# Seven block products in place of eight in the up half of a shared feed-forward network, with operand sums on GpSimd and token routing moved later

## The chip, the cores and the metric

The kernel runs on one core of a Trainium2 chip. The metric is device time in microseconds (us), from the start to the end of one execution. The engines are named as in the profile: PE (TensorE) multiplies matrices, DVE (VectorE) and ACT (ScalarE) work element by element, POOL (GpSimd) does so too and issues gathers and scatters, SP (SyncE) issues the other DMA transfers. Each engine works through its own list of instructions in order and stops at a wait until a semaphore has the value wanted.

## The reference

Inputs are x (2 x 2048 x 512, so 4096 tokens of width 512), a condition vector per batch, and weights. The tokens are first projected by a conditioned 512 x 512 matrix. Then each token goes through a shared two-layer network (512 to 2048 to 512) and through one of two routed networks of the same size, chosen by a gate, and the sums are added to x:

```python
xf = conditioned_projection(x, cond)             # 4096 x 512
top1 = argmax(softmax(xf @ gate_w.T))
shared = relu(xf @ sw1 + sb1) @ sw2 + sb2        # the part that is changed: relu(xf @ sw1 + sb1)
routing = relu(xf @ w1[top1] + b1[top1]) @ w2[top1] + b2[top1]
out = x + routing + shared
```

(Rows of the expert that was not chosen are zero at its input, but still give relu(b1) @ w2 + b2; the kernel adds this as a constant row.)

## The kernel before, in words

Every fp32 product is made of three matmuls: an operand a is split into a high part (rounded to fp32r) and a low part (a minus the high part), and high*high, high*low and low*high are summed. ACT makes the high parts (a cast), DVE the low parts (a subtraction).

The work goes in four stages, one after the other on PE.

1. Projection (line L1722): 32 chunks of 128 tokens, 12 matmuls each. SP loads x into `ring`, ACT and DVE split it, ACT or DVE takes the result from PSUM into `xo`, DVE forms the gate score (L1171), SP stores it to DRAM as xf (L518). Meanwhile the first weights of the shared network are loaded (`raw_load`, L492), cast (`raw_hi`, L834) and subtracted (`raw_lo`, L1201), and the first block of 1024 tokens is read back (`rows`, L524), transposed on DVE (`flip`, L1221) and split into `xw` (`block_hi` L848, `block_lo` L1227).
2. Up half of the shared network (L1776): four blocks s of 1024 tokens, four groups g in each, numbered u = 4s + g from 0 to 15. A group makes relu(xf @ sw1 + sb1) for 4 of the 16 slices of 128 hidden columns. These are two rows (h) by two pairs (p). Together with the two halves (t) of 512 tokens and the two halves (q) of the 512 inputs this is a 2 x 2 by 2 x 2 block product; a group computes it directly, in four steps c (`UP_STEPS`, L79) with 2 x 12 matmuls each. ACT takes each PSUM bank with bias and relu into `vb11`, `vb21`, `vt1` and `vb22` (L932). DVE makes from these the operands of the next stage, t1 to t4, by four subtractions of 128 x 1024 (L1300, L1310, L1263, L1268), and SP stores all seven (512 KB each, L536) to DRAM. In groups 0 to 2 the rest of the weights of sw1 are loaded and split; in groups 8 to 15 (`RAW_JOBS`, L85) those of sw2, with the sums that stage 3 needs. Each block's `rows` are loaded in group g = 1 of the block before (`next_rows`, L528), flipped in g = 2 and split in g = 3 and in the next g = 0. The routing (softmax, choice, counts, places: L1330 to L1418) stands in DVE's list in groups 0 and 1, the scatter of the token table on POOL (L692) in groups 3 to 6.
3. Down half of the shared network (L1811): seven block products per 1024 tokens instead of eight, from the seven stored operands and seven combinations of the weights.
4. The routed networks (L1846, L1870), then the scatter of the results.

PSUM has eight banks, `turn` is four pairs of them. Step c of a group uses pair c, and PE waits before step c only until ACT has taken what step c of the group before left there (L1769). ACT in turn waits for the stores of two groups before (L929) and the subtractions of the group before (L930), since each buffer but `vt3` and `vt4` is there twice.

In the prediction, "c0 to c6" are the seven products of a group of the changed kernel, each with two halves p = 0, 1 of six matmuls.

Of the kernel before, what the change touches and what calls it, by code (L numbers as in the profile page):

```python
# [12 lines left out]
P = 128  # L13
# [15 lines left out]
RAW_AT = (18, 25)  # L29
FLIP_AT = (20, 22, 24, 26)  # L30

LOAD_AT = (4, 20, 27)
ROWS_AT = (10, 12, 14, 16)
# [25 lines left out]
RANK_GROUP = 1  # L59
SCATTER_GROUP = 3  # L60
# [18 lines left out]
UP_STEPS = ((0, 0), (1, 0), (0, 1), (1, 1))  # L79
# [5 lines left out]
RAW_JOBS = {0: (2, 3, 4), 1: (5, 6), 2: (7,), 8: (8, 9), 9: (10,), 10: (11,), 11: (12,), 12: (13, 14), 13: (15, 16, 17), 14: (18, 19),  # L85
            15: (20, 21)}

EARLY = {(3, 4): 0, (3, 7): 1}
# [33 lines left out]
def build(nc, x_rows, x_cols, cond, w_cond, w_shared, w_pack, b1_pack, sb2_cols, b2_rows, gate, out):  # L122
# [4 lines left out]
    with ExitStack() as ctx:  # L127
# [57 lines left out]
        w_raw = at(40, "w_raw", [KD, D])  # L185
        scratch = at(104, "scratch", [KD, D])
        junk = at(38, "junk", [D])
        x_hi = at(128, "x_hi", [KD, T], F32R)
        x_lo = at(136, "x_lo", [KD, T], F32R)
        ring = at(144, "ring", [RING, D])  # L190
# [3 lines left out]
        gate_w = at(96, "gate_w", [2, D])  # L194
        d_rows = at(100, "d_rows", [D])
# [3 lines left out]
        vb11 = [at(kb, f"vb11_{i}", [2, T]) for i, kb in enumerate((128, 56))]  # L199
        vt1 = [at(kb, f"vt1_{i}", [2, T]) for i, kb in enumerate((132, 148))]  # L200
        vb22 = [at(kb, f"vb22_{i}", [2, T]) for i, kb in enumerate((136, 60))]
        vb21 = [at(kb, f"vb21_{i}", [2, T]) for i, kb in enumerate((140, 120))]
        vt2 = [at(kb, f"vt2_{i}", [2, T]) for i, kb in enumerate((144, 124))]
        vt3 = at(204, "vt3", [2, T])
        vt4 = at(200, "vt4", [2, T])
        xw = at(152, "xw", [4, 2, 2, T], F32R)
        rows = at(184, "rows", [JW, QF])
        raw = at(208, "raw", [4, 256])
        raw_last = [at(kb, f"raw_last{i}", [4, 256]) for i, kb in enumerate((160, 164))]
        sums = at(212, "sums", [3, 256])  # L210
        rank = at(104, "rank", [2, NT])
        scan = at(104.5, "scan", [2, NT])
        place = at(105, "place", [4, NT])
        ids = at(106, "ids", [NT * IDW], I32)
# [35 lines left out]


# [6 lines left out]
        raw_in = sem("raw_in")  # L258
        raw_last_in = [sem(f"raw_last_in{i}") for i in range(2)]
# [1749 lines left out]
```

## Time and profile before

| | us |
|---|---|
| median of 3 runs | 1463.8 (1463.56 to 1463.91) |
| span of the profiled execution | 1461.8 |
| projection, to the first up matmul | 97.0 |
| up half, first to last matmul | 97.0 to about 445.7 |
| down half | 445.7 to about 751 |
| routed networks and end | the rest |

Readings of the profile: "busy" is the time that an engine had an instruction in work; "idle before" is the time that it waited in front of a group of instructions, with what ended the wait. The chain is followed back from the last instruction of the kernel, at each step to what released it.

### The profile page before, as it was taken

How to read it: one execution, taken by the hardware profiler on the slowest of the kernel's cores; microseconds unless marked ns; L12 is line 12 of the kernel's file. 1: busy time of each engine (PE TensorE's matmuls, PEld its weight loads, DVE VectorE, ACT ScalarE, POOL GpSimd, SP SyncE). 2: the span in 40 equal slices, each digit the busy share in tenths (PEclk: the TensorE clock that was granted, in tenths of full speed). 3: DMA queues.
4: the chain of work that ended last, by engine and by line, in shares of the span. 5: the costliest groups of instructions: out<-in, count | busy, mean ns of one | idle time of the engine just before them, and what ended most of it. 6: DMA issues, size and time to landing. Idle time of an engine off the chain costs nothing.

```text
span 1461.8 us, 17696 instructions
## 1 busy us (share of the span) xinstructions
PE 1455.4 (100%) x6454; PEld 1207.6 (83%) x6454; DVE 739.2 (51%) x1206; ACT 454.1 (31%) x724; POOL 313.4 (21%) x354
## 2 busy tenths in 40 slices
PE   9999999999999999999999999999999999999998
PEld 8888888888888888888888888888888888888886
DVE  7853723444437877777874514324245531423235
ACT  4353322323336444444533211111124211111112
POOL 0000233210001110000033240614215151340533
PEclk9999999999999999999999999999999999999999
DMA  6947675695678897977675220312106221120312
GB/s 214 283 143 220 222 207 200 194 267 204 213 261 311 283 296 260 288 251 238 204 223 172 60 49 12 66 20 47 40 10 205 60 58 30 29 57 2 66 22 33
DMA packets 157445, 219.87 MB, mean 150 GB/s; under 512 B 46816, under 2 KB 63712, under 8 KB 157376
## 3 DMA queue, kind: packets, MB, share of 16 engines
q1 hardware_dynamic: 142496, 190.90, 40.7%
q0 software_dynamic: 14880, 28.07, 9.5%
q8 instruction: 40, 0.66, 0.2%
q14 instruction: 29, 0.24, 0.0%
HBM read 135.39 MB, written 85.75 MB: 151 GB/s over the span
## 4 chain that ended last, share of the span: by engine, by line
PE 98%; POOL 0%; issue 0%; DVE 0%; DMA 0%; POOLq 0%; DVEq 0%
PE bank L1776 24%; PE bank L1846 24%; PE bank L1870 23%; PE bank L1811 21%; PE bank L1722 6%; PE bank L1866 0%; PE bank L1699 0%; POOL out L735 0%; PE bank L1705 0%; DMA out<-res,tab 0%; POOL out L738 0%; DVE res L1621 0%; POOLq L127 0%; DVE res L1662 0%; DVEq L127 0%
## 5 line engine op out<-in xcount | busy, mean ns | idle before, releaser
L1776 PE MATMUL bank<-xw,w_hi 128*128 128x512 f32 x1024 | 315.5, 389 | 0.0
L718 POOL DMA_INDIRECT rows_e<-xf_scratch,soft x144 | 143.4, 996 | 724.3 <-PE bank L1811 323.3
L1811 PE MATMUL bank<-hl,w_hi 128*128 128x512 f32 x896 | 275.7, 389 | 0.0
L1023 ACT ACTIVATE hf<-bank,b 128x512 f32<-128x512 f32 (+1 forms) x128 | 87.2, 681 | 547.8 <-PE bank L1846 457.6
L1595 DVE CAST h_hi<-hf 128x512 fp32r<-128x512 f32 (+1 forms) x128 | 56.9, 444 | 387.7 <-ACT hf L1023 331.5
L1776 PEld LDWEIGHTS bank<-xw,w_hi 128*128 128x128 f32 x1024 | 192.1, 188 | 39.8
L1776 PE MATMUL bank<-xw,w_lo 128*128 128x512 f32 x512 | 199.2, 389 | 0.0
L1846 PE MATMUL bank<-xe_lo,w_hi 128*128 128x512 f32 (+1 forms) x512 | 197.7, 386 | 0.0
L1846 PE MATMUL bank<-xe_hi,w_hi 128*128 128x512 f32 (+1 forms) x512 | 197.6, 386 | 0.0
L1811 PEld LDWEIGHTS bank<-hl,w_hi 128*128 128x128 f32 x896 | 168.2, 188 | 34.9
L1846 PE MATMUL bank<-xe_hi,w_lo 128*128 128x512 f32 (+1 forms) x512 | 196.0, 386 | 0.0
L1870 PE MATMUL bank<-w_lo,h_hi 128*128 128x512 f32 x496 | 193.0, 389 | 0.0
L1870 PE MATMUL bank<-w_hi,h_hi 128*128 128x512 f32 x496 | 193.0, 389 | 0.0
L1870 PE MATMUL bank<-w_hi,h_lo 128*128 128x512 f32 x496 | 193.0, 389 | 0.0
L898 ACT CAST hl<-hin 128x512 fp32r<-128x512 f32 x224 | 137.6, 621 | 147.2 <-PE bank L1811 123.3
L1256 DVE TENSOR_TENSOR hl<-hin,hl 128x512 fp32r<-128x512 f32 x224 | 147.7, 686 | 63.8 <-ACT hl L898 63.3
L1811 PE MATMUL bank<-hl,w_lo 128*128 128x512 f32 x448 | 174.3, 389 | 0.0
L932 ACT ACTIVATE vb<-bank,b 128x512 f32<-128x512 f32 x96 | 65.7, 690 | 152.0 <-PE bank L1776 149.5
L1776 PEld LDWEIGHTS bank<-xw,w_lo 128*128 128x128 f32 x512 | 96.1, 188 | 20.0
L1846 PEld LDWEIGHTS bank<-xe_lo,w_hi 128*128 128x128 f32 x512 | 96.2, 188 | 18.7
L1846 PEld LDWEIGHTS bank<-xe_hi,w_hi 128*128 128x128 f32 x512 | 96.1, 188 | 18.8
L1846 PEld LDWEIGHTS bank<-xe_hi,w_lo 128*128 128x128 f32 x512 | 96.0, 188 | 18.4
(208 smaller groups left out, 1566.9 us busy)
## 6 DMA issues: line engine op xcount, KB each, us to landing
hin<-hidden_scratch SPq DMA_DIRECT2D x112, 512.0 KB
hidden_scratch<-vt SPq DMA_DIRECT2D x64, 512.0 KB, 3.1
hidden_scratch<-vb SPq DMA_DIRECT2D x48, 512.0 KB, 5.1
stage<-w_pack SPq DMA_DIRECT2D x64, 256.0 KB
raw<-w_shared SPq DMA_DIRECT2D x44, 256.0 KB
ring<-x_cols SPq DMA_DIRECT2D x32, 256.0 KB, 4.2
xf_scratch<-xo SPq DMA_DIRECT2D x32, 256.0 KB, 3.8
rows<-xf_scratch SPq DMA_DIRECT2D x16, 512.0 KB, 9.3
```

The source lines that it names most:

```text
L718: pool.indirect_dma_start(rows_e[:, c % JN, :], None, xf_dram, bass.IndirectOffsetOnAxis(tab_rows[:, c:c + 1], 0)).then_inc(rows_gathered, ...
L898: nc.scalar.copy(hl[:, n % HL, 0, :], hin[:, n // 2 % LOADS, n % 2, :]).then_inc(hu_hi, 1)
L932: nc.scalar.activation(dst[:, p, :], turn[c][p][:], ACT.Relu, bias=b1[:, 0, n:n + 1]).then_inc(up_relu, 1)
L1023: nc.scalar.activation(hf[:, j % 2, 0:width(u)], hidden_bank(j, first and e > 0)[:, 0:width(u)], ACT.Relu, bias=b1[:, 1 + e, j:j + 1]).the ...
L1256: nc.vector.tensor_tensor(hl[:, n % HL, 1, :], hin[:, n // 2 % LOADS, n % 2, :], hl[:, n % HL, 0, :].bitcast(F32), ALU.subtract).then_inc( ...
L1595: nc.vector.tensor_copy(h_hi[:, buf, 0:filled_n], hf[:, j % 2, 0:filled_n]).then_inc(hh_ready, 4)
L1722: last = nc.tensor.matmul(p_ps[c % P_BANKS][:], lhs[:, k, i * P:(i + 1) * P], rhs[:, 24 + 4 * b + k, :], start=(k == 0 and q == 0), stop=( ...
L1776: last = nc.tensor.matmul(turn[c][p][:], w[:, 2 * h + q, 2 * g + p, part], xw[:, 2 * t + q, x, k, :], start=(n == 1), stop=(n == 12))
L1811: last = nc.tensor.matmul(bank[p][:], w[:, DOWN_W[c], i, part], hl[:, n % HL, h, :], start=(i == 0 and q == 0), stop=(i == PAIRS - 1 and q ...
L1846: last = nc.tensor.matmul(hidden_bank(j, change)[:, 0:width(u)], w_of(lhs, lhs3, j, j + 1)[:, 0, part], rhs[:, k, 0:width(u)], start=(k == ...
L1870: last = nc.tensor.matmul(y_ps[m][:], lhs[:, j % HB, part], w_of(rhs, rhs3, j, j + 1)[:, 0, D:2 * D], start=(j == 0 and q == 0), stop=(j = ...
```

## The change

The up half is computed by seven block products per group instead of eight. With b11, b12, b21, b22 for the blocks of x, the kernel makes four sums of them on POOL (`x_sums`), and three sums of the weight blocks (`raw_sums`, also moved from DVE to POOL). Each product c has its own split operand in `xw` (seven of them, not four, so seven `block_hi` and `block_lo` per block), and six matmuls per half, not twelve. Products 0, 2, 4 and 6 of a group run into one and the same pair of banks (`UP_BANK`), without clearing it: ACT takes the bank after 0, after 2 and after 6, DVE adds what stands there after 4 to `vb22`; 1 and 5 share a second pair, 3 has a third. So the results are no longer taken with relu directly: ACT takes 0, 1 and 2 with the bias alone, DVE adds products 3, 4 and 5 to them from PSUM (`add`, six of 128 x 512), ACT applies relu to `vb11` and `vb22` in place (two of 128 x 1024), and relu for `vt1` is within t1's subtraction. `vt1`, `vb22`, `vb21` and `vt2` are there only once; t3 is made in place in `vb11`, t4 in `vb21`.

Before c2 PE waits for ACT's take of c0, before c4 for that of c2, before c5 for that of c1, before c6 for DVE's add of c4, and before c3 for DVE's add of c5 in the group before.

Weights of sw1 and sw2 are now loaded once each into the first buffer (16 loads, not 22). The choice of the expert moves to group 4, the counting to group 5, the places to group 8, the scatter to groups 9 to 11 and the reading of the table to group 12. In the projection, loads, flips and splits come at other chunks, and buffers move to other addresses.

Most lines that are only removed are left out of the diff; they stand in the functions above.

```diff
-RAW_AT = (18, 25)
-FLIP_AT = (20, 22, 24, 26)
-LOAD_AT = (4, 20, 27)
-ROWS_AT = (10, 12, 14, 16)
+RAW_AT = (13, 17)
+FLIP_AT = (18, 19, 20, 21)
+X_AT = (22, 24, 26, 28, 30)
+LOAD_AT = (4, 14, 18)
+ROWS_AT = (9, 11, 12, 13)
...
-RANK_GROUP = 1
-SCATTER_GROUP = 3
+CHOOSE_GROUP = 4
+RANK_GROUP = 5
+PLACE_GROUP = 8
+SCATTER_GROUP = 9
+TABLE_GROUP = 12
...
-UP_STEPS = ((0, 0), (1, 0), (0, 1), (1, 1))
+UP_BANK = (0, 1, 0, 2, 0, 1, 0)
+FRESH = (0, 1, 3)
+PER_GROUP = 2 * STEPS
+X_ORDER = (0, 1, 3, 2, 4, 5, 6)
+X_DONE = tuple(X_ORDER.index(c) + 1 for c in range(STEPS))
+X_EARLY = 5
+X_SUM = (None, 1, 3, None, 2, None, 4)
...
+RAW_JOBS = {0: (2, 3), 1: (4, 5), 2: (6, 7), 13: (8, 9), 14: (10, 11), 15: (12, 13)}
+RAW_FIRST = {0: (4,), 1: (6,), 12: (8, 9), 13: (10, 11), 14: (12, 13)}
+RAW_SECOND = {0: (3,), 1: (5,), 2: (7,)}
...
+                home = RAW_HOME[n]
+                if RAW_USE[n]:
+                    before_n = max(m for m in range(n) if RAW_HOME[m] == home)
+                    sp.wait_ge(raw_ready, before_n + 1)
+                    sp.wait_ge(sums_made, 4 * (before_n + 1))
...
+                    last = u == GROUPS * BLOCKS - 1
+                    if last:
+                        for n in range(LOADS - 1):
+                            hidden_load(n)
+                    if u > 0:
+                        keep_t3(u - 1)
                     if g == 1 and s < BLOCKS - 1:
                         next_rows(s)
+                    for n in RAW_SECOND.get(u, ()):
+                        raw_load(n)
                     if u > 0:
...
+                        keep_t4(u - 1)
+                    sp.wait_ge(b11_made, u + 1)
                     keep(vb11[u % 2][:], s, g, 0).then_inc(b11_out[u % 2], DMA)
...
+                    sp.wait_ge(b22_made, u + 1)
+                    keep(vb22[:], s, g, 5).then_inc(b22_out, DMA)
+                    for n in RAW_FIRST.get(u, ()):
                         raw_load(n)
...
+            def x_sums(s):
+                b11_x, b12_x, b21_x, b22_x = half_of(0, 0), half_of(0, 1), half_of(1, 0), half_of(1, 1)
+                pool.wait_ge(x_flip, FLIPS * (s + 1))
+                pool.wait_ge(xw_lo, STEPS * s + X_DONE[0])
+                pool.tensor_tensor(b11_x, b12_x, b11_x, ALU.subtract).then_inc(x_sum, 1)
+                pool.wait_ge(x_sum, 4 * s + 1)
+                pool.tensor_tensor(b12_x, b22_x, b12_x, ALU.subtract).then_inc(x_sum, 1)
+                pool.wait_ge(xw_lo, STEPS * s + X_DONE[1])
+                pool.tensor_tensor(b11_x, b22_x, b11_x, ALU.subtract).then_inc(x_sum, 1)
+                pool.wait_ge(x_sum, 4 * s + 3)
+                pool.wait_ge(xw_lo, STEPS * s + X_DONE[3])
+                pool.tensor_tensor(b21_x, b21_x, b11_x, ALU.subtract).then_inc(x_sum, 1)
+            for n in range(3):
+                raw_sums(n)
+            x_sums(0)
+            for n in range(3, PAIRS):
+                raw_sums(n)
+            x_sums(1)
...
             pool.wait_ge(pads_out, 2 * DMA)
...
+            def block_hi(s, i):
+                c = X_ORDER[i]
                 act.wait_ge(x_flip, FLIPS * (s + 1))
+                if X_SUM[c]:
+                    act.wait_ge(x_sum, 4 * s + X_SUM[c])
                 if s > 0:
...
+                    act.wait_ge(up_mm, PER_GROUP * (GROUPS * s - 1) + 2 * c + 2)
                 nc.scalar.copy(in_blocks(xw[:, c, 0, :, :]), X_OF[c]).then_inc(xw_hi, 1)
             act.wait_ge(fills_made, 2)
...
+                def take(dst, c, h, f):
                     for p in range(2):
...
+                        nc.scalar.activation(dst[:, p, :], up_bank(u, UP_BANK[c])[p][:], f, bias=b1[:, 0, n:n + 1]).then_inc(up_kept, 1)
+                if u == CHOOSE_GROUP:
                     act.wait_ge(soft_in, 3)
                     nc.scalar.activation(soft[:, 3:5, :], soft[:, 1:3, :], ACT.Exp).then_inc(soft_exp, 1)
+                wait(act, t3_out[u % 2], DMA * (u // 2))
+                take(vb11[u % 2], 0, 0, ACT.Identity)
+                if g == 0:
+                    for i in range(X_EARLY, STEPS):
+                        block_hi(s, i)
+                if more:
+                    block_hi(s + 1, 0)
                 for n in jobs[:1]:
                     raw_hi(n)
...
+                take(vb22, 1, 1, ACT.Identity)
+                for n in jobs[:1]:
+                    raw_sums_hi(n)
+                if last:
+                    first_units(0, 2)
+                wait(act, t1_out, DMA * u)
+                take(vt1, 2, 0, ACT.Identity)
...
+                for n in jobs[1:]:
                     raw_hi(n)
                 if last:
...
+            def make_t1(u):
+                dve.wait_ge(b11_made, u + 1)
+                dve.wait_ge(up_added, 6 * u + 6)
+                nc.vector.scalar_tensor_tensor(out=vt1[:], in0=vt1[:], scalar=0.0, in1=vb11[u % 2][:], op0=ALU.max,
+                                               op1=ALU.subtract).then_inc(ht_made, 1)
+            def make_t2(u):
+                dve.wait_ge(b22_made, u + 1)
+                dve.wait_ge(ht_made, 4 * u + 1)
+                wait(dve, t2_out, DMA * u)
+                nc.vector.tensor_tensor(vt2[:], vb22[:], vt1[:], ALU.subtract).then_inc(ht_made, 1)
...
+                dve.wait_ge(b11_out[u % 2], DMA * (u // 2 + 1))
                 dve.wait_ge(ht_made, 4 * u + 2)
...
             def make_t4(u):
...
+                dve.wait_ge(b21_out, DMA * (u + 1))
+                dve.wait_ge(up_kept, 8 * u + 8)
+                nc.vector.tensor_tensor(vb21[:], vb21[:], vt2[:], ALU.subtract).then_inc(ht_made, 1)
...
+                more = g == GROUPS - 1 and s < BLOCKS - 1
+                def add(dst, c, kept, p):
+                    dve.wait_ge(up_mm, PER_GROUP * u + 2 * c + p + 1)
+                    dve.wait_ge(up_kept, 8 * u + kept + p + 1)
+                    nc.vector.tensor_tensor(dst[:, p, :], up_bank(u, UP_BANK[c])[p][:], dst[:, p, :], ALU.add).then_inc(up_added, 1)
+                if u == CHOOSE_GROUP:
+                    softmax_start()
+                if g == 0:
+                    for i in range(X_EARLY, STEPS):
+                        block_lo(s, i)
...
+                for n in jobs[:1]:
+                    raw_lo(n)
+                    raw_sums_lo(n)
+                if u == CHOOSE_GROUP:
...
+                    slots()
+                if u == PLACE_GROUP:
                     places()
...
+                if u > 0:
+                    make_t4(u - 1)
+                if more:
                     block_lo(s + 1, 0)
                     block_lo(s + 1, 1)
...
+                if last:
+                    units_lo(0, 2)
+                add(vb11[u % 2], 3, 0, 0)
+                add(vb11[u % 2], 3, 0, 1)
+                for n in jobs[1:]:
+                    raw_lo(n)
+                add(vb22, 4, 2, 0)
+                if more:
+                    block_lo(s + 1, 2)
+                add(vb22, 4, 2, 1)
+                if more:
+                    block_lo(s + 1, 3)
+                for n in jobs[1:]:
+                    raw_sums_lo(n)
+                add(vt1, 5, 4, 0)
+                add(vt1, 5, 4, 1)
+                if more:
+                    block_lo(s + 1, 4)
                 if u == 0:
                     for i in range(RING):
                         dve.wait_ge(xf_out[i], DMA * NT // RING)
...
+                if last:
+                    units_lo(2, 4)
+                make_t1(u)
+                if last:
+                    raw_lo(RAW_LAST)
...
+                            pe.wait_ge(raw_ready, pair + 1)
+                        if s == 0 and c == 2:
+                            pe.wait_ge(sums_ready, pair + 1)
+                        if c == 0:
+                            wait(pe, up_added, 6 * (u - 2) + p + 1)
+                        elif c == 1:
+                            wait(pe, up_kept, 8 * (u - 1) + 6 + p + 1)
+                        elif c == 2:
+                            pe.wait_ge(up_kept, 8 * u + p + 1)
+                        elif c == 3:
+                            wait(pe, up_added, 6 * (u - 1) + 4 + p + 1)
+                        elif c == 4:
+                            pe.wait_ge(up_kept, 8 * u + 4 + p + 1)
+                        elif c == 5:
+                            pe.wait_ge(up_kept, 8 * u + 2 + p + 1)
+                        else:
+                            pe.wait_ge(up_added, 6 * u + 2 + p + 1)
                         n = 0
...
+                        for k in range(2):
+                            part = slice(k * P, (k + 1) * P)
+                            for w, x in ((w8_hi, 0), (w8_hi, 1), (w8_lo, 0)):
+                                n += 1
+                                last = nc.tensor.matmul(up_bank(u, UP_BANK[c])[p][:], w[:, DOWN_W[c], pair, part], xw[:, c, x, k, :],
+                                                        start=(c in FRESH and n == 1), stop=(n == 6), skip_group_check=(c not in FRESH))
                         last.then_inc(up_mm, 1)
                     if u == RANK_GROUP and c == 0:
```

## Rows read from the trace of the kernel before

**Rows 1.** The page: the span and each engine's busy time, share, instructions

```profile
span 1461.8 us, 17696 instructions
...
PE 1455.4 (100%) x6454; PEld 1207.6 (83%) x6454; DVE 739.2 (51%) x1206; ACT 454.1 (31%) x724; POOL 313.4 (21%) x354
```

**Rows 2.** Waits of PE: engine, line waited for, us, times, longest

```profile
PE bank L1699 <- POOL ones L664: 1.2, 1, 1.2
```

**Rows 3.** The chain that ended last: start us, length us, what ran

```profile
1.19 4.33 PE bank L1699 x10
...
124.77 321.09 PE bank L1776 x1416
```

**Rows 4.** Line L1776: duration ns min/median/max, first and last start us, forms

```profile
L1776 PE MATMUL bank<-xw,w_hi x1024: 387/389/477, 97.0 to 445.2; 128*128 128x512 f32 x171
...
L1776 PE MATMUL bank<-xw,w_lo x512: 389/389/397, 97.5 to 445.5; 128*128 128x512 f32 x171
```

**Rows 5.** Groups by shape: operation, shapes, count, busy us, mean ns, idle, releaser

```profile
L932 ACT ACTIVATE vb<-bank,b 128x512 f32<-128x512 f32 x96 | 65.7, 690 | 152.0 <-PE bank L1776 149.5 <-DVE vt L1310 2.0
...
L1310 DVE TENSOR_TENSOR vt<-vb,vt 128x1024 f32<-128x1024 f32 x16 | 19.6, 1225 | 48.8 <-ACT vb L932 48.6
...
L1225 DVE STREAM_TRANSPOSE rows<-rows 128x1024 f32<-128x1024 f32 x16 | 18.8, 1220 | 0.0
...
L1210 DVE TENSOR_TENSOR w_lo<-raw,w_hi 128x1024 fp32r<-128x1024 f32 x14 | 17.2, 1225 | 36.8 <-ACT w_hi L838 27.1 <-ACT w_hi L846 9.4
L853 ACT CAST xw<-rows 128x1024 fp32r<-128x1024 f32 x16 | 16.1, 1047 | 0.0
L1488 DVE TENSOR_TENSOR v<-bank,v 128x512 f32<-128x512 f32 x24 | 15.4, 684 | 0.3
...
L1210 DVE TENSOR_TENSOR w_lo<-sums,w_hi 128x768 fp32r<-128x768 f32 x8 | 7.7, 958 | 7.2 <-ACT w_hi L841 7.2
...
L706 POOL TENSOR_SCALAR soft<-soft 128x144 int32<-128x144 int32 x1 | 0.7, 697 | 0.1
...
L686 POOL IOTA ids<- 128x512 int32 x1 | 0.7, 656 | 32.1 <-DVE w_lo L1158 32.1
```

**Rows 6.** Groups of POOL in 0 to 110 us

```profile
L673 POOL IOTA order<- 128x32 f32 x1 | 0.2, 156 | 0.0
```

**Rows 7.** ACT in order of time, first block group: start us, us, engine, line

```profile
100.04 0.69 ACT L932 ACTIVATE vb<-bank,b 128x512 f32<-128x512 f32 x1 [1.27 <-PE bank L1776]
...
103.39 1.28 ACT L940 ACT_TABLE_LOAD   x1
104.68 0.26 ACT L940 ACTIVATE soft<-soft 128x64 f32<-128x64 f32 x1
...
142.48 1.05 ACT L838 CAST w_hi<-raw 128x1024 fp32r<-128x1024 f32 x1 [11.41 <-DMA raw<-w_shared]
```

**Rows 8.** DVE in order of time, the routing steps

```profile
124.80 0.22 DVE L1351 COPY rank<-bank 128x64 f32<-128x64 f32 x1 [1.36 <-PE bank L1785]
...
144.70 0.15 DVE L1392 TENSOR_SCALAR filled<-scan 128x1 f32<-128x1 f32 x1
...
151.78 0.19 DVE L1408 TENSOR_TENSOR place<-scan,rank 128x32 f32<-128x32 f32 x1
...
158.06 1.22 DVE L1300 TENSOR_TENSOR vt<-vt,vb 128x1024 f32<-128x1024 f32 x1
```

**Rows 9.** SP in order of time: start us, us of issuing, what

```profile
119.68 6.42 SPq L532 DMA_DIRECT2D rows<-xf_scratch  x4
...
131.60 1.10 SPq L507 DMA_DIRECT2D raw<-w_shared  x2
```

**Rows 10.** Windows of 2 us: PE, PEld, DVE, ACT, POOL, PEclk, DMA share, GB/s

```profile
131.00:133.00 2.00, 2.00 (x11) 1.65 (x10) 0.00 (x0) 0.06 (x1) 0.00 (x0) 1.00 1.22 218
133.00:135.00 2.00, 2.00 (x11) 1.65 (x10) 0.00 (x0) 0.00 (x0) 0.00 (x0) 1.00 1.02 382
```

**Rows 11.** Line L536, the stores of halves: us from issue to landing

```profile
DMA to landing us min/median/max: 2.8/3.5/11.6
```

More of the change, by code:

```diff
@@ L249, in down_bank, with up_bank, wc_tile, sums_of @@
             return turn[(STEPS * s + c) % TURN]
+        def up_bank(u, role):
+            return turn[(3 * u + role) % TURN]
+        def wc_tile(b, k):
+            return 28 + k if b else 4 * k + 3
+        def sums_of(n):
+            return sums if n < 2 * PAIRS - 1 else sums_last
         const_in = sem("const_in")
@@ L942, in up_group @@
                     raw_hi(n)
-                relu(vb21[u % 2], b21_out, 1)
-                for n in jobs[1:2]:
-                    raw_hi(n)
-                if s < BLOCKS - 1 and g == GROUPS - 1:
-                    block_hi(s + 1, 0)
+                wait(act, b22_out, DMA * u)
+                wait(act, ht_made, 4 * (u - 1) + 2)
+                take(vb22, 1, 1, ACT.Identity)
[3 more added lines that the diff above has]
+                    first_units(0, 2)
@@ L958, in _ @@
+                if last:
+                    first_units(6, HL)
+                if u == 0:
+                    for i in range(RING):
+                        act.wait_ge(xf_out[i], DMA * NT // RING)
+                wait(act, t4_out, DMA * u)
+                take(vb21, 6, 1, ACT.Relu)
             act.wait_ge(tile_mm, NT)
@@ L1272, in up_group @@
                 jobs = RAW_JOBS.get(u, ())
-                b11, b21, b22, t1, t2 = (x[u % 2] for x in (vb11, vb21, vb22, vt1, vt2))
-                if s > 0 and g == 0:
-                    block_lo(s, 2)
-                    block_lo(s, 3)
-                for n in jobs[:2]:
-                    if n == PAIRS - 1:
-                        raw_job(n)
-                if s < BLOCKS - 1 and g == 2:
+                last = u == GROUPS * BLOCKS - 1
+                more = g == GROUPS - 1 and s < BLOCKS - 1
@@ L1300, in up_group @@
[L1300 to L1310 removed]
+                if last:
+                    units_lo(0, 2)
@@ L1359, in count, with slots @@
                     a = 1 - a
-            def places():
+            def slots():
                 total = scan[:, 1, NT - 1:NT]
@@ L1764, in up_group @@
                         pe.wait_ge(rank_kept, 1)
                     for p in range(2):
+                        pair = 2 * g + p
                         if s == 0 and c == 0:
[L1768 to L1777 removed]
+                            pe.wait_ge(raw_ready, pair + 1)
```

445 lines of the change are left out of this document (192 added, 253 removed).

## The prediction

> **What bounds the kernel now.** First the page: PE is busy for 1455.4 of 1461.8 us [rows 1]. Then its waits, to see whether that is real work: its only wait is 1.2 us at the start [rows 2]. Then the chain that ended last: in the up half it is PE alone, 1416 matmuls in 321.09 us, 0.2268 us each [rows 3] (the 389 ns of a single matmul [rows 4] overlap with the next). Six matmuls take 1.36 us, twelve 2.72. So PE's instruction count sets the time, and whatever else happens between 97 and 446 us is hidden. The question is what stops being hidden.
>
> **What goes.** A group had 4 x 2 x 12 = 96 matmuls and will have 7 x 2 x 6 = 84; over 16 groups 1536 [rows 4] become 1344. 192 x 0.2268 = 43.5 us less, if PE never waits. A group then lasts 84 x 0.2268 = 19.05 us. The stages before and behind keep their matmuls. Six weight loads and DVE's weight sums go too; they were hidden, 0.
>
> **What comes, in a plain group.** I count from the group's start; product cj ends at 2.72(j+1), its first half 1.36 earlier, and ACT or DVE start about 0.3 us later (the first take began at 100.04, 2.72 + 0.3 behind 97.0 [rows 7]). Prices: a take 0.69, an add from PSUM 0.68, a DVE operation of 128x1024 1.22, of 128x768 0.96, an ACT cast of 128x1024 1.05 [rows 5]; I take relu in place at 1.05 too.
> ACT: 8 takes and 2 relus = 7.6 us of 19.05, before 5.5. DVE: 6 adds and 4 subtractions = 9.0, before 4.9. Both fit; the order counts, as PE now waits within the group. Take c0 ends at 2.4, needed at 5.44; take c2 at 7.8, needed at 10.9; add of c4's first half at 13.2, needed by c6 at 16.3. Everywhere about 3.1 us in hand, where before it was nearly a whole group (ACT once sat 11.41 us on a load [rows 7], and PE never noticed [rows 2]). Ahead of the adds in DVE's list is t4 of the group before, which waits for b21's store: taken at 20.05, so 1.0 into the next group, landing 3.5 us later [rows 11], t4 ends at 5.8; c3's add is due from 9.8. t1 is stored at about 18.7 and lands at 22.2, 3.2 into the next group, where ACT wants the buffer at 7.1. In groups 5 and 9 t4's store stands behind `rows` in SP's list (t3 at 2.1, rows to about 13), lands by 16, and ACT wants the buffer at 18: 0. The single buffers cost nothing at 3.5 us. So a plain group costs 0; what follows are the groups with extra work.
>
> **Projection, 0.** Five block splits and two pairs of weight splits in place of four and two, on engines that PE leads by up to four chunks (10.9 us).
>
> **Group 0, 0.3 us.** Weight load 3 goes out when `raw_lo(2)` is done (8.6), lands at 12, two sums on POOL (0.7 each, below), cast 1.05, subtraction 1.22, then the add for c6: 16.3 to 16.7 against 16.3.
>
> **Group 1, 7 us.** SP issues t3's store, then the four `rows` loads, then weight load 5. t3 of group 0 is made at about 23, 4 into group 1. The rows run at 205 to 218 GB/s until 133 us and the stores behind them at 382 [rows 10]; 2.1 MB are 10 us. In the kernel before, the load issued at 131.60 behind rows issued from 119.68 [rows 9] was there only at 142.48 [rows 7], 22.8 us after the first rows, with some 7 stores besides (1.3 us each). Here about 2 us of stores, 10 of rows and 1.3 + 1.4 of its own: it lands 15 us after 4, at about 19. Two sums, cast, `raw_lo(5)` and the add follow (1.4 + 1.05 + 1.22 + 0.7), 23.3, against 16.3: 7 us. `raw_lo(5)` stands in DVE's list before c4's add, and `raw_hi(5)` in ACT's before the relus, so all of them wait. Bounds 4 (t3 earlier, queue empty) and 10 (queue full).
> **Group 2, 1.3 us.** DVE is 4 us late, then 4 flips (4.9), split of 6, load 7 out at 9.9, landing 13.3, the same 4.4: 17.7 against 16.3.
>
> **Change of block (groups 3, 7, 11), 0 in the group itself, but DVE ends late.** Five of seven splits are made in the old block's last group, with POOL's sums between. The trace has no POOL operation with two inputs. Nearest rows: iota takes 156 ns for 32 columns and 656 for 512 [rows 5, 6], 1.04 ns a column; with two inputs I take twice that, 2.3 us for 1024 and 0.7 for 256. Bounds: 1.2 (as DVE) and 5 (the int32 TENSOR_SCALAR, 697 ns for 144 columns [rows 5], scaled). With 2.3: block split 0 ends at 7.0, sum 1 at 9.3, its cast 10.4, its subtraction 11.6, sum 3 at 13.9, and the last split at 18.9; t1, t2, t3 end at 22.6, 3.6 into the next group. PE's operands are all in time (c1 of the next block at 21.8, c2 at 24.5). If instead DVE's subtractions and POOL's sums don't overlap but take turns, each chain link grows by up to 1.2 to 2.3, and DVE ends 7.0 late. No row shows two-input work of both at a time; I take the middle, 5.3.
> The Trainium skill, "SBUF — State Buffer", section "Who interferes with whom", says that a DVE instruction with two SBUF inputs and a GpSimd instruction that reads SBUF lock each other out; by it the lateness is 7.0 and the sum 3.5 us larger, 1439; without it 2.7 us less. Its page "GPSIMD Engine Reference" (section "Elementwise — side-by-side cycle accounting") gives 4497 ns for 2048 columns, an estimate of 2.25 us here. No run here shows either yet.
>
> **Group 4, 2.7 us.** ACT's list begins with the Exp, which waits for DVE's `softmax_start`, which stands behind t3: 5.3 + 0.5, then table load and Exp 1.28 + 0.26 [rows 7], then take c0: 8.1 against 5.44 for c2. Bounds 1.0 and 9 (POOL at 5 us).
> **Group 5, 0.2.** Count about 2.0 from 124.80, `slots` 7.1 (144.70 to 151.78) [rows 8], from 3.9 on; then t4 and three adds: 16.3 to 16.5.
> **Group 8, 1.0.** 5.3 late, splits 5 and 6 (2.4), places 6.3 (151.78 to 158.06 [rows 8]), t4 1.2, three adds 2.1: 17.3 against 16.3. Bounds 0 and 7.4.
> **Scatter, table, weights of sw2, 0**: POOL only, or 4.4 us of DVE per group with 7 us free, no rows in the queue from group 12 on.
> **Into the down half, 0.3.** Unit 6 is split at 26.7 against 27.2, unit 7 at 28.6 against 28.6.
> **Clock, 2.1.** After idleness the first ten matmuls took 4.33 us in place of 2.27 [rows 3], 2.1 more. I charge that once, for the 7 us gap; 0 and three times are the bounds.
>
> **Sum.** 0.3 + 7 + 1.3 + 2.7 + 0.2 + 1.0 + 0.3 + 2.1 = 14.9. Span 1461.8 - 43.5 + 14.9 = 1433.2. The median of the runs stands 2.0 above the span: 1435.2.
>
> **Rivals.**
> *The covers hold.* The weight load overtakes or t3 comes early, POOL is fast: 0 to 8 us lost, 1463.8 - 43.5 + 4 = 1424. For it: 3 us in hand everywhere and an unloaded store of 3.5 us. Against: SP's order in group 1 is fixed.
> *DVE and POOL take turns* (the rule above): DVE ends block changes 7.0 late, group 4 loses 4.5 and group 8 2.8, 1438.8; if they overlap in full 3.6 late, 1.1 and 0, 1432.5. For the first: the chain cast, subtraction, sum leaves them back to back; against: no row has them together. I hold them equally likely; both lie within the forecast's case.
> *POOL is slow.* At 5 us a sum DVE ends block changes 11.7 late: group 4 loses 9, group 8 7.4, three block changes 4 together, with the 8.9 of groups 0 to 2, 5 and the end, and three clock prices 6.3: 36 us, 1456. For it: the int32 row. Against: that row has few columns, much of it may be fixed.
> *Slower: the single buffers bind in every group.* b21's store must land before t4, t4 precedes the adds: 1.1 + L + 1.2 + 2.1 reaches 16.3 at a landing L of 11.9 us. Each us beyond costs 16, so from L = 14.6 on the gain is gone; L = 16 gives 1463.8 - 43.5 + 4.1 x 16 = 1486. For it: the same bytes in less time, and a largest landing of 11.6 [rows 11]. Against: the median is 3.5, and a group's stores need 7 x 1.3 = 9 of 19 us.
>
> **Chances.** Forecast (1428 to 1444) 0.50, half of it with turns, half without; covers hold (1420 to 1428) 0.28; slow POOL (1444 to 1462) 0.15; binding stores 0.07. The forecast is the first. The range 1422 to 1450 holds it, most of the second and the near part of the third. 0.2% (3 us) is about what a measurement can tell from no change: faster 0.92; same 0.02, from the ends of the last two cases; slower 0.06.
>
> **What would show it.** 1344 matmuls in the up half at 0.2268 us; PE's waits: one of 5 to 10 us in group 1, ended by a DVE add behind `raw_lo`, one of 1 to 5 in group 4, near 189 us, in front of c2, ended by ACT's take, one of up to 3 in group 8; plain groups 6, 9, 10 and 13 to 15 at 19.05 us. POOL's 128x1024 sums at 2.3 us; 3.5 us landing for the stores. Wrong would be: no wait in group 1 (the queue isn't in order, or t3 earlier), waits in each group (stores or ACT's length), or sums of over 3 us.

## The result and the profile after

| | before | after |
|---|---|---|
| median of the runs | 1463.9 us (1463.6 to 1463.9) | 1507.0 us (1504.9 to 1510.9) |
| ratio to before, 95% interval | | 1.0296 [1.0284, 1.0309] |
| span of the profiled execution | 1461.8 us | 1504.9 us |
| PE busy, matmuls | 1455.4 us, 6454 | 1428.1 us, 6262 |
| mean granted clock | 1.00 | 0.978 |

The change made the kernel 3% slower; 1435.2 was forecast, in 1422 to 1450. The page of the profile shows that the matmuls went, and the tenths show where the time came back.

```profile
span 1504.9 us, 17708 instructions
...
PE 1428.1 (95%) x6262; PEld 1177.5 (78%) x6262; DVE 830.8 (55%) x1282; ACT 502.0 (33%) x776; POOL 406.9 (27%) x434
...
PE   9897889999549999999999999999999999999998
```

PE's instructions fell by 192 as planned, yet its busy time fell only from 1455.4 [rows 1] to 1428.1, 27.3 us in place of 43.5. The third line is PE's busy share in 40 slices of 37.6 us: the "54" are the slices from 376 to 451 us, about half empty. The waits of PE (engine, line, what it waited for: us in total, times, longest):

```profile
PE bank L1889 <- ACT vt L998: 35.7, 3, 35.4
PE bank L1889 <- DVE vb L1356: 20.6, 8, 11.0
PE bank L1889 <- ACT vb L998: 4.9, 2, 3.4
PE bank L1926 <- DVE hl L1317: 4.6, 1, 4.6
PE bank L1817 <- DVE x_lo L1180: 4.3, 1, 4.3
```

Before, the only wait was the 1.2 us at the start [rows 2]. Together with one of 0.2 these are 70.3 us. PE in order of time shows the five longest (start, us, what, and in brackets the idle time before it and its releaser):

```profile
74.53 0.79 PE L1817 MATMUL bank<-w_hi,x_hi 128*128 128x512 f32 x1 [4.28 <-DVE x_lo L1180]
...
154.42 1.22 PE L1889 MATMUL bank<-xw,w_hi 128*128 128x512 f32 x2 [11.02 <-DVE vb L1356]
...
209.28 1.19 PE L1889 MATMUL bank<-xw,w_hi 128*128 128x512 f32 x2 [3.39 <-ACT vb L998]
...
432.77 1.22 PE L1889 MATMUL bank<-xw,w_hi 128*128 128x512 f32 x2 [35.35 <-ACT vt L998]
...
492.09 1.15 PE L1926 MATMUL bank<-hl,w_hi 128*128 128x512 f32 x2 [4.64 <-DVE hl L1317]
```

They are the projection, group 1, group 4, group 13 and the start of the down half.

**The account closes.** Without any loss the span would be 1461.8 - 43.5 = 1418.3, with PE busy for 1455.4 - 43.5 = 1411.9. Whatever PE waits for comes on top, and so does what its busy time exceeds 1411.9 by. After: 70.3 of waits and 1428.1 - 1411.9 = 16.2 of excess give 1504.8; the span is 1504.9. This is bookkeeping: PE is either busy or waits, so the account must close. What it gives is the split into waits and slower work, and it is used for every run below.

What the excess is, the windows show (PE, PEld, DVE, ACT, POOL, then PEclk, the DMA share and GB/s):

```profile
432.00:434.00 2.00, 1.23 (x3) 1.04 (x4) 1.84 (x2) 1.29 (x3) 0.74 (x1) 0.50 0.00 0
434.00:436.00 2.00, 2.00 (x6) 1.52 (x6) 1.45 (x3) 0.26 (x1) 1.84 (x3) 0.50 0.45 161
436.00:438.00 2.00, 2.00 (x7) 1.58 (x6) 1.18 (x1) 2.00 (x3) 1.20 (x2) 0.60 0.29 110
```

The granted clock is 0.50, the 1.2 GHz level, at the end of group 13's wait and for some 4.8 us behind it, and 1.00 (2.4 GHz) in a plain group. At 0.50 PE starts a matmul every 0.43 us in place of 0.227, so 4.8 us there cost 47% of that, 2.3. The same windows behind the other long gaps show 0.50 for 4.7 us (projection), 3.3 (group 1), 3.0 (group 4), 3.0 (group 8, behind a gap of 2.73) and 3.5 (down half). Behind the gap of 2.33 in group 0 it stays at 1.00. By the same 47% the six cost 10.5 us, an estimate. The other 5.7 of the excess I have not divided further; in e11 below, where the mean granted clock is 1.000, 5.4 us of excess are left, which points to a part of about that size that is not the clock.

### The profile page after: what moved, and what is told of

It is laid out like the page before. It is cut to its first block, busy times and chain, and to the rows that moved or that the text cites. A ratio compares the mean times of both kernels' runs of the same rounds, so it can differ in the third digit from the quotient of the medians.

```text
span 1504.9 us, 17708 instructions
## 1 busy us (share of the span) xinstructions
PE 1428.1 (95%) x6262; PEld 1177.5 (78%) x6262; DVE 830.8 (55%) x1282; ACT 502.0 (33%) x776; POOL 406.9 (27%) x434
## 4 chain that ended last, share of the span: by engine, by line
PE 71%; issue 4%; DVE 2%; DMA 2%; POOL 2%; ACT 0%; POOLq 0%; SPq 0%; DVEq 0%; ACTq 0%
PE bank L1961 23%; PE bank L1985 22%; PE bank L1926 20%; PE bank L1889 5%; DMA hin<-hidden_scratch 1%; POOL soft L770 1%; PE bank L1981 0%; DVE xw L1290 0%; DMA hidden_scratch<-vb 0%; DMA soft<-token_table 0%; DVE vb L1356 0%; DVE vt L1332 0%; POOL out L804 0%; POOL tab L767 0%; DVE vt L1324 0%
## 5 line engine op out<-in xcount | busy, mean ns | idle before, releaser
L1889 PE MATMUL bank<-xw,w_hi 128*128 128x512 f32 x896 | 282.9, 397 | 61.3 <-ACT vt L998 35.7
L1889 PEld LDWEIGHTS bank<-xw,w_hi 128*128 128x128 f32 x896 | 170.3, 192 | 102.5 <-ACT vt L998 36.4
L1889 PE MATMUL bank<-xw,w_lo 128*128 128x512 f32 x448 | 176.5, 394 | 0.0
L1985 PEld LDWEIGHTS bank<-w_hi,h_lo 128*128 128x128 f32 x496 | 93.1, 188 | 19.3
L1985 PEld LDWEIGHTS bank<-w_lo,h_hi 128*128 128x128 f32 x496 | 93.2, 188 | 19.2
```

What stands on the lines that cost most here:

```text
L1889: last = nc.tensor.matmul(up_bank(u, UP_BANK[c])[p][:], w[:, DOWN_W[c], pair, part], xw[:, c, x, k, :], start=(c in FRESH and n == 1), sto ...
L1985: last = nc.tensor.matmul(y_ps[m][:], lhs[:, j % HB, part], w_of(rhs, rhs3, j, j + 1)[:, 0, D:2 * D], start=(j == 0 and q == 0), stop=(j = ...
```

## What held group 13

POOL in order of time, from the end of the last `x_sums` on:

```profile
367.77 1.30 POOL L767 DMA_DIRECT2D tab<-token_table  x1
372.27 1.18 POOL L770 DMA_DIRECT2D soft<-token_table  x1 [3.20 <-issue]
...
417.77 1.12 POOL L770 DMA_DIRECT2D soft<-token_table  x1 [3.44 <-issue]
421.81 0.33 POOL L774 TENSOR_SCALAR tab_in<-tab 128x36 int32<-128x36 int32 x1 [2.93 <-DMA soft<-token_table]
...
427.58 0.72 POOL L723 TENSOR_TENSOR sums<-raw 128x256 f32<-128x256 f32 x1 [2.08 <-issue]
428.38 0.72 POOL L725 TENSOR_TENSOR raw<-raw 128x256 f32<-128x256 f32 x1
```

And ACT behind it:

```profile
429.19 1.04 ACT L914 CAST w_hi<-raw 128x1024 fp32r<-128x1024 f32 x1 [39.21 <-POOL raw L725]
```

Ten reads of the token table, issued by POOL (each takes 2304 single numbers of 4 bytes out of rows of 64), are each busy for 1.1 to 1.3 us, and between one and the next lie 3 to 7 us with nothing that the profile shows to wait for ("issue"): 54 us from the first to the table's use. In the kernel before the same ten were issued from 250 to 303 us, hidden. Its first and its last:

```profile
249.96 1.28 POOL L698 DMA_DIRECT2D tab<-token_table  x1 [1.42 <-DMA token_table<-ids,pos]
...
302.71 1.12 POOL L701 DMA_DIRECT2D soft<-token_table  x1 [8.83 <-issue]
```

Now the sums of the sw2 weights, which group 13 is the first to need, are behind them in POOL's list. ACT's cast waits 39 us for them and holds the takes behind it, and PE waits 35 us for a bank that only a take empties. No engine is overloaded here (POOL is 27% busy); it is the order of one list.

## Experiments

No run leaves out part of the computation. Medians, ratios to the kernel before on the same chip, and the account:

| run | median us | ratio [95%] | PE waits | excess | 1418.3 + both | span |
|---|---|---|---|---|---|---|
| after | 1507.0 | 1.0296 [1.0284, 1.0309] | 70.3 | 16.2 | 1504.8 | 1504.9 |
| e1 | 1470.2 | 1.0032 [1.0019, 1.0046] | 34.4 | 14.6 | 1467.3 | 1467.4 |
| e2 | 1503.7 | 1.0278 [1.0261, 1.0295] | 66.9 | 15.8 | 1501.0 | 1501.0 |
| e3 | 1497.5 | 1.0229 [1.0212, 1.0246] | 59.9 | 16.3 | 1494.5 | 1494.8 |
| e4 | 1459.5 | 0.9971 [0.9961, 0.9980] | 30.4 | 15.1 | 1463.8 | 1463.8 |
| e5 | 1451.6 | 0.9906 [0.9884, 0.9928] | 19.9 | 13.3 | 1451.5 | 1451.4 |
| e6 | 1454.1 | 0.9938 [0.9922, 0.9954] | 21.1 | 13.5 | 1452.9 | 1453.0 |
| e7 | 1451.8 | 0.9915 [0.9898, 0.9932] | 21.8 | 13.3 | 1453.4 | 1453.5 |
| e8 | 1498.2 | 1.0223 [1.0202, 1.0244] | 62.4 | 15.3 | 1496.0 | 1496.2 |
| e9 | 1441.5 | 0.9840 [0.9827, 0.9853] | 11.9 | 8.3 | 1438.5 | 1438.6 |
| e10 | 1440.4 | 0.9835 [0.9822, 0.9848] | 14.9 | 6.6 | 1439.8 | 1440.0 |
| e11 | 1443.5 | 0.9868 [0.9850, 0.9886] | 14.1 | 5.4 | 1437.8 | 1438.0 |

(PE waits without the 1.2 us at the start, which the kernel before has too. Waits, excess and span are those of the one execution that was profiled, which need not be a typical one: e4's is the slowest of its ten, 1465.8 us against a median of 1459.5, e11's the fastest of its four. Single waits also differ between runs whose code is the same up to them: the wait in the projection is 4.28 us in the changed kernel, 5.79 in e1 and 4.58 in e3. A difference of some 3 us between two medians is within the intervals.)

### e1: the weight sums ahead of the table reads

```diff
+            for n in range(PAIRS, 2 * PAIRS):
+                raw_sums(n)
-            pool.wait_ge(up_mm, PER_GROUP * TABLE_GROUP)
 ...
-            for n in range(PAIRS, 2 * PAIRS):
-                raw_sums(n)
```

> The changed kernel with one edit: POOL makes the sums of the sw2 weights (n = 8 to 15) before it reads the token table back, not after. Theory A (POOL's order is the cause): ACT's first weight cast of group 13 waited for POOL, which was busy with ten table reads from 367.8 to 421.7 us, and PE waited 35.35 us behind it and then ran some 6 us at the lower clock. Without it the wait is gone: 1507 - 35 - 3 = 1469, and no PE wait over 5 us after group 8. Rival B (the weight loads themselves are late, held by the scatter or by the stores in the queue): 1500 to 1507, the wait stays with POOL's first sum ended by a DMA. Rival C (the table is then late for the gathers of the routed networks): the wait is gone in the up half but one of 10 to 40 us comes at the start of the routed part, 1480 to 1507.

The edit also drops the wait that held the reads until group 12; it could not bind any more, since the reads now come behind the last sums, at 450 us. POOL of this run:

```profile
387.51 1.14 POOL L723 TENSOR_TENSOR sums<-raw 128x256 f32<-128x256 f32 x1 [20.25 <-DMA raw<-w_shared]
...
450.47 1.30 POOL L768 DMA_DIRECT2D tab<-token_table  x1
```

Measured 1470.2. The first sum is 40 us earlier than in the changed kernel (427.58), as soon as its load is there. PE's waits fall from 70.3 to 34.4; the one of 35 us is gone, and the only one that grew by more than 0.3 us is that of the projection (4.28 to 5.79), which the edit does not touch. This one order costs 37 us, nearly half of the 86.6 that the span lost against 1418.3. Theory A holds. Rival B falls, since the load was there at 387, and rival C too: the reads run to after 500 us now, and no wait of PE comes in the routed part.

### e2: weight load 1 ahead, in the projection

```diff
-RAW_AT = (13, 17)
+RAW_AT = (13, 20)
-LOAD_AT = (4, 14, 18)
+LOAD_AT = (4, 14, 21)
```

> The changed kernel with the second weight split of the projection three chunks later (chunk 20, not 17) and the third load behind it (21, not 18). Theory A (load 1 stands in the queue behind the four rows loads, ACT waits 6.10 us for its sums and holds up x's split): the 4.28 us wait of PE at 74.5 and the slow clock behind it go, first up matmul at 97 to 98, 1507 - 7 = 1500. Rival B (DVE is held up by POOL's x sums, the gate score took 2.89 us beside one): the start of the up half stays at 103 to 104.5, 1505 to 1507.

Measured 1503.7, not clear of noise against 1507.0. The wait at 74.5 us went, and one of 5.1 us came 20 us later. PE, POOL and DVE of this run:

```profile
95.04 0.79 PE L1817 MATMUL bank<-w_hi,x_hi 128*128 128x512 f32 x1 [5.09 <-DVE x_lo L1180]
```

```profile
85.38 0.73 POOL L723 TENSOR_TENSOR sums<-raw 128x256 f32<-128x256 f32 x1 [12.15 <-DMA raw<-w_shared]
...
88.52 2.36 POOL L736 TENSOR_TENSOR rows<-rows 128x1024 f32<-128x1024 f32 x1
90.95 2.35 POOL L738 TENSOR_TENSOR rows<-rows 128x1024 f32<-128x1024 f32 x1
```

```profile
92.04 2.34 DVE L1290 TENSOR_TENSOR xw<-rows,xw 128x1024 fp32r<-128x1024 f32 x1 [6.73 <-ACT xw L929]
94.31 0.68 DVE L1180 TENSOR_TENSOR x_lo<-ring,x_hi 128x512 fp32r<-128x512 f32 x1
```

POOL waits 12 us for load 2, with the block sums behind it; their cast on ACT, the subtraction on DVE and then the projection's own split wait in turn. The up half began at 105.2 us, no earlier than the 104.5 of the changed kernel, so theory A's gain did not come. Rival B's reason is not shown by that either, as the wait is another one now. The load was not the whole cause, the order of POOL's list was the other part. The wait was real, the edit moved it.

### e3: weight load 5 ahead of the rows, in group 1

```diff
+                    for n in RAW_SECOND.get(u, ()):
+                        raw_load(n)
                     if g == 1 and s < BLOCKS - 1:
                         next_rows(s)
-                    for n in RAW_SECOND.get(u, ()):
-                        raw_load(n)
```

> The changed kernel, but in the second group of a block SP issues the next weight load before the four rows loads. Theory A (the rows loads delayed weight load 5 and with it DVE's add for product 6): PE's wait of 11.0 us in group 1 shrinks to 0 to 2, and the slow clock behind it (about 2 us) goes: 1507 - 12 = 1495. Rival B (the queue is full of stores whatever the order, and the later rows make the flips of group 2 late): 3 to 8 us come back in group 2, 1499 to 1505.

Measured 1497.5, 9.5 us less. Group 1's wait falls from 11.02 to 1.75 us:

```profile
146.32 0.74 PE L1889 MATMUL bank<-xw,w_hi 128*128 128x512 f32 x2 [1.75 <-DVE vb L1356]
```

The cause named in the prediction, the load behind the rows in SP's list, is shown. A part of rival B is there too: group 2 waits 2.8 us now (0.74 and 2.05), where it waited 0.3.

### e4: the three together

> All three edits together. If the three losses are independent they add: 1507 - 38 - 7 - 12 = 1450, 14 us below the kernel before, ratio 0.99. If one hides behind another (a group that starts earlier meets the same late transfer), 1455 to 1465. What is left over the ideal 1420 is then the waits of groups 0, 3, 4, 8, 11 and at the start of the down half with their slow clock, about 27 us.

Measured 1459.5, 0.3% below the kernel before. One by one the gains are 36.8, 3.3 and 9.5, 49.6 in sum, and together 47.5: within the noise they add. The case of 1450 had expected 57 us of single gains, so 1459.5 falls into the range of its rival without showing that one loss hides behind another. What is left is 30.4 us in gaps of 0.7 to 5.2 each, so no single cause.

### e5: three more

POOL's `x_sums(0)` ahead of `raw_sums(2)` (what e2 lacked), the Exp behind the first takes of group 4, and unit 6's split behind `raw_hi(14)` in the last group.

```diff
-            for n in range(3):
+            for n in range(2):
                 raw_sums(n)
             x_sums(0)
 ...
                 take(vb22, 1, 1, ACT.Identity)
+                if u == CHOOSE_GROUP:
+                    act.wait_ge(soft_in, 3)
+                    nc.scalar.activation(soft[:, 3:5, :], soft[:, 1:3, :], ACT.Exp).then_inc(soft_exp, 1)
 ...
             raw_hi(RAW_LAST)
+            first_units(6, HL)
             raw_hi(RAW_LAST + 1)
```

> The three edits of before and three more: POOL makes block 0's x sums ahead of the sums of weight 2 (in the run with the later loads PE's wait of the projection had only moved, to ACT behind POOL, which waited for load 2); in group 4 ACT's Exp stands behind the takes of products 0 and 1; and ACT splits unit 6 of the down half only behind the last take and cast 14. Theory: each of the three waits that are left there goes with its slow clock: projection 5 to 7 + 2, group 4 3.4 + 1.9, start of the down half 4.0 + 2: 1459.5 - 18 = 1441. Rival (they are covers of each other, the next one comes up at once): 1450 to 1458.

Measured 1451.6, inside the rival's range and 10 above mine. The three gaps aimed at went or shrank: group 4's 3.38 is gone, the projection's 6.6 us of waits are 0.6, the down half's 4.0 is 2.07 and 0.58. What else is left are gaps that were not aimed at (PE in order of time). The first was 1.48 us in e4, the second 2.72 as here, the third is new:

```profile
120.91 0.70 PE L1887 MATMUL bank<-xw,w_hi 128*128 128x512 f32 x2 [3.58 <-DVE vb L1354]
...
285.24 0.88 PE L1887 MATMUL bank<-xw,w_hi 128*128 128x512 f32 x2 [2.72 <-DVE vb L1354]
...
328.84 0.73 PE L1887 MATMUL bank<-xw,w_hi 128*128 128x512 f32 x2 [3.65 <-issue]
```

### e6: the places one group later

```diff
-PLACE_GROUP = 8
+PLACE_GROUP = 9
```

> As the run before, and DVE computes the places in group 9, not 8. Theory: the wait of 2.7 us in group 8, ended by DVE's add, is due to 6.3 us of small steps on top of a late DVE; in group 9 DVE is not late: 2.7 + 1.9 less, 1436 to 1437. Rival: POOL's scatter then starts later and its x sums of the last block come late, so group 11 waits 2 to 8 us more, 1440 to 1446.

Measured 1454.1, nothing gained. The wait of group 8 (2.72) went, and three of 2.81, 1.39 and 4.71 us came between 314 and 332 us, in group 10. These are the subject of e11.

### e7 and e8: the sums of x on DVE

The four operand sums of each block go from POOL to DVE, behind the block splits they read; e7 is e6 with it, e8 the changed kernel with nothing else.

```diff
-            x_sums(0)
...
+            def x_sum_part(s, k):
...
+                nc.vector.tensor_tensor(out, a, b, ALU.subtract).then_inc(x_sum, 1)
...
+                for k in {0: (0, 1), 1: (2,), 2: (3,)}.get(i, ()):
+                    x_sum_part(s, k)
```

> As the run before, and the four x sums of each block are made on DVE, each right behind the split it needs, none on POOL. It measures the disputed cost: POOL takes 2.4 us for each and DVE's two-input work beside it grew from 1.22 to 2.4 and 3.1. Theory (they take turns, so POOL's help costs DVE as much as doing it itself, and the links are longer): DVE work of 1.22 us instead, the waits of 1.5 + 0.7 us in the groups of block change go, 2 to 6 us less than the run before. Rival (POOL's sums are mostly hidden and DVE, the fuller engine, gets 4.9 us more per block): 2 to 8 us more.

> The changed kernel with that edit alone (x sums on DVE). If POOL's slowness and its turns with DVE were what made the change slow, it gains 20 us or more: 1485. If, as the trace says, the time went mainly to the table read, 1500 to 1507: at most the 2 us waits of three block changes and half of group 4's.

e7 measured 1451.8, e8 1498.2: 2.3 us less than e6, and 8.9 less than the changed kernel, between my two cases and next to the smaller gain. The 8.9 us are clear of noise, the 2.3 are not. So in the changed kernel DVE with four more operations per block loses less than with POOL doing them. What speaks for turns taken, DVE and POOL of the changed kernel show:

```profile
101.16 2.89 DVE L1262 CUSTOM_DVE_ANT_0 junk<-xo,gate_w 128x512 f32<-128x512 f32 x1
...
104.21 0.69 DVE L1262 CUSTOM_DVE_ANT_0 junk<-xo,gate_w 128x512 f32<-128x512 f32 x1
```

```profile
100.78 2.72 POOL L743 TENSOR_TENSOR rows<-rows 128x1024 f32<-128x1024 f32 x1 [3.05 <-DVE xw L1290]
```

```profile
196.33 1.80 DVE L1290 TENSOR_TENSOR xw<-rows,xw 128x1024 fp32r<-128x1024 f32 x1
198.05 0.68 DVE L1356 TENSOR_TENSOR vb<-bank,vb 128x512 f32<-128x512 f32 x1
198.65 3.09 DVE L1290 TENSOR_TENSOR xw<-rows,xw 128x1024 fp32r<-128x1024 f32 x1
201.67 1.28 DVE L1356 TENSOR_TENSOR vt<-bank,vt 128x512 f32<-128x512 f32 x2
202.87 1.21 DVE L1290 TENSOR_TENSOR xw<-rows,xw 128x1024 fp32r<-128x1024 f32 x1
```

The same gate product takes 2.89 us beside a sum of POOL and 0.69 without; the same subtraction 3.09 and 1.21. The adds, which read PSUM, keep their 0.68. With the sums on DVE, group 4's wait falls from 3.39 to 1.49 and group 8's from 2.73 to 0.83. The edit does two things, though: it ends the turns, and it takes the x sums out of POOL's list, where others stand behind them. The run doesn't divide the 8.9 us between the two. It also has a new gap of 2.63 us put down to "issue", of the kind of the one in e5:

```profile
324.85 0.73 PE L1881 MATMUL bank<-xw,w_hi 128*128 128x512 f32 x2 [2.63 <-issue]
```

### e9 and e10: back to group 8 for the places, and a later scatter

e9 is e5 with the x sums on DVE; e10 is e9 with

```diff
-SCATTER_GROUP = 9
+SCATTER_GROUP = 10
```

> The six moved pieces as in the run at 1451.6, places of the rows in group 8 as there, and x sums on DVE. Theory A (moving the places to group 9 was what cost 2.5 us, since the trace of that run shows PE idle 2.81, 1.39 and 4.71 us between 317 and 332 us, and x sums on DVE give back about 2 to 3 us): 1448 to 1449. Rival B (x sums on DVE only help where GpSimd would have locked DVE at the late group changes, and cost as much at the projection): 1451.6, no difference.

> As the run beside it, with GpSimd's 32 scatters of the token table started one group later (group 10). Without the scatter beside it, PE had no idle of 2.6 to 3.7 us put down to 'issue' near 325 to 329 us. Theory A (that idle, in which DVE, ACT and SP stand too, comes from the scatters): it goes or moves about 22 us later, to 347 to 352 us. Rival B (it belongs to the stores of group 9 and 10): it stays at its place. The time: within 3 us of the run beside it, lower by up to 5 us if the idle goes altogether.

e9 measured 1441.5, 22 us below the kernel before and 6.5 below my better case; neither theory had its size. Against e7, which has the places in group 9, it is 10.4 us less. The account says where the 10 us against e5 are: 8.0 of waits and 5.0 of excess, in the profiled execution 12.8. Of the gaps shown for e5, the one at 121 us is 0.65 now, the one at 285 us is 0.80, the one at 329 is gone. So the x sums on POOL cost time in groups 0 and 8, where I had not expected it. Whether the gap at 329 us belongs to them is open: in e9 the scatters, too, start 6.8 us earlier than in e5 (see e11). e10 measured 1440.4, no difference clear of noise, and since e9 had no "issue" gap it could not show where that one comes from.

### e11: places in group 9 with the later scatter

> Six pieces moved, x sums on DVE, the places of the rows in group 9 (1451.8 us so, with the scatters in group 9) and the scatters now from group 10. The open point is the stall of 304 to 332 us of that run (PE idle 2.8, 0.7 and 5.0 us there, ACT and DVE waiting for banks or for nothing the profile names), which the run at 1441.5 with the places in group 8 does not have. Theory A (it comes from the 32 scatters running beside the first half of group 9 and the stores of group 9): gone, 1441 to 1444. Rival B (it comes from the places standing in group 9 themselves, 6.3 us of DVE ahead of its adds there): stays, 1450 to 1453.

e11 is e7 with the scatters from group 10 on, and e10 with the places in group 9. The stall in e7, PE and DVE:

```profile
332.11 1.22 PE L1879 MATMUL bank<-xw,w_hi 128*128 128x512 f32 x2 [5.04 <-DVE vb L1346]
```

```profile
330.77 1.89 DVE L1346 TENSOR_TENSOR vb<-bank,vb 128x512 f32<-128x512 f32 x3 [4.92 <-remote]
```

Measured 1443.5, 8.3 us below e7 and clear of noise: in the profiled execution the stall is gone with the places still in group 9. So the places in group 9 are not enough to cause it, and the time at which the scatters run has a part in it. Part only: e9 has the 32 scatters in groups 9 to 11 as well, and no stall. The first scatter starts at 290.65, 292.86, 293.93 and 298.15 us in e5, e6, e7 and e8, which have a gap of this kind, and at 283.90, 304.18 and 301.12 in e9, e10 and e11, which do not, nor do the changed kernel and e1 to e4 (299.85 to 308.13). In e7 DVE waits 4.92 us and POOL itself 3.5 for "remote", by which the profile names a releaser that is none of this core's engines. What that is, stays open.

It may also come and go in one and the same kernel. The four executions of e5 took 1446.7 to 1453.9 us, with a mean granted clock of 0.998 in the fastest and 0.993 in the profiled one; those of e11 took 1439.8 (the profiled one, clock 1.000) to 1447.4 us (0.995). Only one execution of each has a trace, so that e11 never has the stall is not shown.

## The prediction step by step

Forecast and measured loss against 43.5 us of gain (span 1418.3):

| step | forecast | measured |
|---|---|---|
| plain groups | 0 | 0 (groups 5 to 7, 9, 10, 12, 14) |
| projection | 0 | 4.3 |
| group 0 | 0.3 | 2.3 |
| group 1 | 7 | 11.0 |
| group 2 | 1.3 | 0.3 |
| change of block, PE's waits | 0 | 5.8 (groups 3 and 11) |
| group 4 | 2.7 | 3.4 |
| group 8 | 1.0 | 2.7 |
| scatter, table, weights of sw2 | 0 | 35.4 |
| into the down half | 0.3 | 4.6 |
| clock (measured: whole excess) | 2.1 | 16.2 |
| group 5 and others | 0.2 | 0.4 |
| sum | 14.9 | 86.4 |

Right: the pace of the matmuls and the count of them; that a plain group has no wait, so that the single buffers don't bind and the slower rival named in the prediction did not occur (the time was slower for another reason); the waits in groups 1, 4 and 8, with their place and their releaser; the price of POOL's sums, 2.47 to 2.48 us for 1024 columns against 2.3 and 0.80 to 1.02 for 256 against 0.7.

**The step that failed is "Scatter, table, weights of sw2, 0: POOL only".** It counted POOL's busy time and left out POOL's order. The ten reads are in the kernel before as well, from 250 us on, with 3.1 to 8.8 us of idle "issue" between them, and I read no row of them because nothing waited for them. The diff puts the sums of the sw2 weights behind them in the same list, where before no weight depended on POOL at all. e1 shows it: 36.8 us for this order alone. Half of the 71.8 us between forecast and result is this step. Without it the kernel takes 1470.2, still outside the forecast range; the other half is in the terms below.

**Clock, 2.1.** Mis-sized. I charged it once, for the one gap that I took to be long. The rows show 0.50 behind six gaps, the shortest 2.73 us, and the estimate from the windows is 10.5. It grows with the number of gaps, so each term with a gap of that size lacked 1.4 to 2.3 us, by the same estimate.

**Projection, 0.** Wrong for the same reason as the main step. "Engines that PE leads by up to four chunks" counts work, but the x split waits in DVE's list behind a weight split, which waits for POOL, which waits for a load that SP issued at 60 us. e2, where the later load moved the wait behind POOL's list, shows that both hold it.

**Group 1, 7.** Right in mechanism, e3 shows it; measured 11.0, above my upper bound of 10. The load went out at 139.5, 8.1 us behind the rows, as these issues took 8.08 us in place of 6.42 [rows 9], and POOL had it at 149.55, 22.7 us into the group where 19 was forecast. The issuing is 1.7 of these 3.7 us; the rest I have not divided:

```profile
131.35 8.08 SPq L561 DMA_DIRECT2D rows<-xf_scratch  x4
139.53 3.34 SPq L539 DMA_DIRECT2D raw<-w_shared  x2
```

```profile
149.55 0.72 POOL L723 TENSOR_TENSOR sums<-raw 128x256 f32<-128x256 f32 x1 [15.88 <-DMA raw<-w_shared]
```

**Change of block.** I took the middle of "turns" and "no turns", 5.3 us late; DVE was done with t3 at 207.9, some 7.6 us into group 4, a little beyond the end with turns (7.0), and PE waited 3.4 us there, between the 2.7 of the middle and the 4.5 of the turns. The Trainium skill, "SBUF — State Buffer", section "Who interferes with whom", says that the two lock each other out when DVE has two SBUF inputs; the rows above agree (0.69 to 2.89 beside 2.72 on POOL), and the 0.68 of the adds that read PSUM agree with it too. I had weighed it at even chances; that it slowed the gate products in the projection, I had not counted at all. From the figure in the Trainium skill's page "GPSIMD Engine Reference" (section "Elementwise — side-by-side cycle accounting") I had estimated 2.25 us for a sum of 1024 columns; 2.47 to 2.48 were measured.

**Into the down half, 0.3.** The split of unit 6 stands in ACT's list ahead of a take and of `raw_hi(14)`, and waited 7.63 us for its load, so what I had timed on its own held the rest. e5, which moves it, leaves 2.7 of e4's 4.0 us.

## What to carry to other kernels

When work that PE needs is given to an engine that was idle, read that engine's whole list in time, with the gaps between its instructions and not its busy share: what stands ahead of the new work was free before and is not now. When the change takes the slack out of a bound engine, many gaps of 1 to 5 us come at once, and each of the longer ones is followed by some 3 to 5 us at half the clock; mend them by the order of the lists, and by which engine does a piece, before giving up the change: the same arithmetic went from 3.0% slower to 1.6% faster here. Elementwise sums given to GpSimd to spare a DVE that is half busy can cost more than they save: moved to DVE they were worth 9 and 10 us in two kernels (with the stall above coming in one and going in the other) and 2 us, within the noise, in a third.

## What the runs showed of the hardware that I had not expected

Reads of single numbers from rows in DRAM, issued by GpSimd, cost its list 4.0 to 7.9 us apiece, 54 us for ten, with no wait shown. A gap of 2.73 us on PE was enough for a granted clock of 0.50 behind it, for 3 us, and so was one of 2.63 in e8; behind 2.33, and 2.44 in e4, it stayed at 1.00. The custom gate product of DVE goes from 0.69 to 2.89 us beside a GpSimd sum. And the stalls near 304 to 332 us in e5 to e8, which the profiled executions show when the scatters start between 290.65 and 298.15 us and not at 283.90 or from 299.85 on, are unexplained.
